# A two-layer AdaLN / Hyena / GQA / MoE kernel: queries and keys projected with features on partitions, and each head's operands fetched by way of HBM

## What is computed

```python
q = (hidden_states @ Wq).reshape(b, s, H, D).transpose(0, 2, 1, 3)
k = (hidden_states @ Wk).reshape(b, s, HKV, D).transpose(0, 2, 1, 3)
v = (hidden_states @ Wv).reshape(b, s, HKV, D).transpose(0, 2, 1, 3)
q = _apply_rope(q, cos, sin)          # re = xe*cos - xo*sin, ro = xe*sin + xo*cos
k = _apply_rope(k, cos, sin)
scores = jnp.einsum('bkgqd,bkpd->bkgqp', qg, k) * scale
scores = jnp.where(causal, scores, jnp.float32(-1e+30))
probs = jax.nn.softmax(scores, axis=-1)
out = jnp.einsum('bkgqp,bkpd->bkgqd', probs, v).reshape(b, H, s, D)
out = out.transpose(0, 2, 1, 3).reshape(b, s, H * D)
return out @ Wo
```

## Time and profile before

| | |
|---|---|
| median of 3 executions | 2249.2 us (2247.33 to 2249.74) |
| the profiled execution | 2249.1 us, its span 2247.3 us |
| mean granted TensorE clock | 0.931 |
| PE busy, weight loads busy | 1951.0 us (87%), 1739.9 us (77%) |
| DVE, ACT, POOL busy | 1338.3 (60%), 829.1 (37%), 508.1 us (23%) |
| moved by DMA | 70.77 MB |

### The profile page before, as it was taken

The page is one execution under the profiler, slowest core; times in us unless marked ns, Lnnn a source line. Parts: engine busy times, 40 slices in busy tenths (PEclk is TensorE's granted clock), DMA queues, the critical chain, the costliest instruction groups (busy, mean ns, idle before and its releaser), DMA issues.

```text
span 2247.3 us, 32490 instructions
## 1 busy us (share of the span) xinstructions
PE 1951.0 (87%) x11892; PEld 1739.9 (77%) x11892; DVE 1338.3 (60%) x3102; ACT 829.1 (37%) x1673; POOL 508.1 (23%) x991
## 2 busy tenths in 40 slices
PE   6868799999876789999976879999987688999997
PEld 4657699999755788999865769989976577999896
DVE  4598555553558755555358865555454985655535
ACT  1303444543321345445231334454422034444423
POOL 0051222121134221221016122212112421222101
PEclk8988899999988889999988889999998798999998
DMA  5400000000410000000050000000041000000005
GB/s 208 178 1 1 1 1 1 1 1 1 168 48 1 1 1 1 1 1 2 13 204 0 1 1 1 1 1 2 1 164 53 1 1 1 1 1 2 1 1 187
DMA packets 28522, 70.77 MB, mean 31 GB/s; under 512 B 4607, under 2 KB 19775, under 8 KB 24774
## 3 DMA queue, kind: packets, MB, share of 16 engines
q1 hardware_dynamic: 28358, 68.60, 8.3%
HBM read 58.35 MB, written 9.98 MB: 30 GB/s over the span
## 4 chain that ended last, share of the span: by engine, by line
PE 60%; DVE 20%; ACT 6%; issue 5%; DVEq 4%; DMA 2%; POOL 2%; POOLq 1%; SPq 1%; ACTq 0%
PE ps L454 20%; PE ps L300 8%; DVE ps L961 6%; PE ps L610 5%; PE ps L423 5%; PE ps L441 4%; PE ps L440 4%; PE ps L306 4%; PE ps L633 3%; PE ps L402 2%; ACT qhh L696 2%; DVE prod L1021 2%; DVE hrow L867 1%; DMA gate_scratch<-grow 1%; DVEq L1043 1%
## 5 line engine op out<-in xcount | busy, mean ns | idle before, releaser
L454 PEld LDWEIGHTS ps<-v,pT 128*128 128x128 f32 x4608 | 546.0, 192 | 12.6 <-ACT pT L713 1.9
L454 PE MATMUL ps<-v,pT 128*128 128x65 f32 x4608 | 538.4, 272 | 1.5 <-ACT pT L713 1.5
L713 ACT ACTIVATE pT<-ps 128x512 f32<-128x512 f32 (+3 forms) x768 | 332.7, 493 | 344.5 <-PE ps L441 332.7
L961 DVE CUSTOM_DVE_ANT_0 ps<-ps,mrow 128x128 f32<-128x128 f32 (+7 forms) x512 | 373.2, 784 | 39.5 <-PE ps L423 39.5
L1173 POOL TENSOR_SCALAR_AFFINE_SELECT pT<-pT 128x128 f32<-128x128 f32 x512 | 145.4, 292 | 928.7 <-ACT pT L713 922.9
L440 PE MATMUL ps<-qhh,khl 128*128 128x512 f32 (+3 forms) x768 | 275.8, 363 | 9.2 <-DMA q<-nmr 9.2
L441 PE MATMUL ps<-q,k 65*128 65x512 f32 (+3 forms) x768 | 261.9, 354 | 0.0
L423 PE MATMUL ps<-khl,qhh 128*128 128x512 f32 (+3 forms) x768 | 228.4, 379 | 36.9 <-DVE mx L961 14.8
L971 DVE RECIPROCAL den<-ps 128x4 f32<-128x4 f32 x128 | 23.4, 183 | 299.8 <-PE ps L454 299.8
L954 DVE TENSOR_TENSOR q<-ps,qhh 64x512 fp32r<-64x512 f32 x128 | 87.4, 683 | 186.6 <-ACT qhh L696 186.6
L672 ACT ACTIVATE hfull<-ps,modb 128x512 f32<-128x512 f32 x48 | 37.3, 776 | 434.4 <-PE ps L378 434.4
(11 more groups left out here) (162 smaller groups left out, 2854.4 us busy)
## 6 DMA issues: line engine op xcount, KB each, us to landing
sgn<-sgn_scratch SPq DMA_DIRECT2D x8, 1024.0 KB, 13.7
Kf<-kf_scratch SPq DMA_DIRECT2D x4, 2048.0 KB, 17.1
in_w<-in_w_scratch SPq DMA_DIRECT2D x4, 1536.0 KB, 10.7
x<-in_x SPq DMA_DIRECT2D x5, 1024.0 KB, 5.4
xn<-in_x SPq DMA_DIRECT2D x4, 1024.0 KB, 7.4
out<-x SPq DMA_DIRECT2D x4, 1024.0 KB, 5.0
wraw<-in_wmod SPq DMA_DIRECT2D x2, 1536.0 KB, 6.7
fwd<-in_fwd SPq DMA_DIRECT2D x5, 512.0 KB, 18.3
```

The source lines that it names most:

```text
L454: q = mm(ps[:, b, (i % 4) * (HD + 1):(i % 4 + 1) * (HD + 1)], pT[:, slot, i * P - lo:(i + 1) * P - lo], v1[:, g % 2, j, :], start=j == 0, ...
L713: A(pT[:, n % PRING, 0:(c + 1) * HALF - lo], ps[:, b, 0:(c + 1) * HALF - lo], ACT.Exp, scale=SCALE)\
L961: V.tensor_tensor_reduce(out=v, in0=v, in1=mrow[:, L - n:L], scale=1.0, scalar=-3e38, op0=ALU.add, op1=ALU.max, accum_out=mx[:, u % 2, i:i ...
```

## The change

1. The weights are laid out so that 128 output features are one half (even or odd rotary halves) of four heads: `project(k, col)` makes 128 features x 512 tokens, two such blocks (`e` = 0, 1) for a turn k, with 12 matmuls of 512 columns. Turns 0 and 2 are the keys of all four groups, turns 1 and 3 the queries of group 0, turns 4 to 9 those of groups 1 to 3; the latter are made during heads 1, 5 and 9. The values of all groups are projected in the prologue (`project_values`, 256 columns).
2. DVE multiplies a block by cosine and sine in one operation of 128x1024, POOL combines with two of 128x512, ACT (`high`) and DVE (`low`) split with one of 128x1024 each. All intermediate space is `oT`, `pT` and a tile `split`.
3. SP stores each turn (1 MB) into `q_scratch` or `k_scratch` in HBM and loads from there what a head needs: three DMAs of 256 KB for a query, 512 and 256 KB for a key. The loads for head u+1 wait until head u-1's exponentials are done, and stand ahead of head u's row of maxima on SP's queue. All transposes of queries and keys are gone, and so are ACT's and DVE's operations for single heads.
4. Storage: the rotary table grows from 256 KB to 1 MB, `zT`, `gabs` and `gsgn` move into other tiles, and two of the Hyena part's three product buffers become `hrow` and `vrow`; the second pooled product therefore waits for the last spectrum (`bk.wait(dve, ("vf", NB - 1))`).

```diff
+            def project(k, col):
+                for e in range(2):
+                    b = bk.take(pe, ("rope", k, e), until=(s["rope_a"], 2 * k + e + 1))
+                    h, c = k % 2 if k >= 4 else k // 2, col + e * P
+                    split_mm(ps[:, b, :], lambda a, q: wqkv[:, a, q, c:c + P],
+                             lambda a, q: hT[:, a, q, h * HALF:(h + 1) * HALF], ND).then_inc(ready[b], 1)
...
-                if i % 4 == 0:
-                    pe.wait_ge(s["q_done"], NHALF * u + i // 4 + 1)
-                    pe.wait_ge(s["k_lo_done"], NHALF * g + i // 4 + 1)
+                if u == 0 and i == 0:
+                    pe.wait_ge(s["first_loaded"], 16 * 5)
+                elif i == (0 if u else 4):
+                    pe.wait_ge(*q_loaded(u))
+                    if u % GQ == 0:
+                        pe.wait_ge(*k_loaded(g))
...
+            def high(k):
+                act.wait_ge(s["rope_done"], k + 1)
+                if k >= 3:
+                    act.wait_ge(*rope_stored({3: 0, 4: 2}.get(k, k - 1)))
+                A(split_of(k)[:, 0], turned(k)[:, 0:2, :], ACT.Copy).then_inc(s["rope_hi"], 1)
...
+            def low(k):
+                dve.wait_ge(s["rope_hi"], k + 1)
+                V.tensor_tensor(split_of(k)[:, 1], turned(k)[:, 0:2, :], split_of(k)[:, 0].bitcast(F32), ALU.subtract)\
+                    .then_inc(s["rope_lo"], 1)
...
+                def store(k):
+                    sp.wait_ge(s["rope_lo"], k + 1)
...
+                    dma(to.rearrange("x p n -> p x n"), split_of(k).rearrange("p a e n -> p (a e) n").bitcast(F32))\
+                        .then_inc(rope_stored(k)[0], 16)
+                def load_key(g, cols, done):
+                    one = k_scratch[:, g * 32:(g + 1) * 32, cols]
+                    dma(khl[:, g % 2, cols].bitcast(F32), one)\
+                        .then_inc(done, 16)
+                    dma(k2[0:HD, g % 2, cols].bitcast(F32), one[0:2]).then_inc(done, 16)
+                def load_query(u, cols, done):
+                    g, j, r = u // GQ, u % GQ, u % QRING
+                    one = q_scratch[g % 2, :, j * 32:(j + 1) * 32, cols]
+                    for half in (0, HD):
+                        dma(qhh[half:half + HD, r, cols].bitcast(F32), one[0:2]).then_inc(done, 16)
+                    dma(q2[0:HD, r, cols].bitcast(F32), one[2:4]).then_inc(done, 16)
+                for h in range(NHALF):
+                    cols = slice(h * HALF, (h + 1) * HALF)
+                    store(2 * h)
+                    store(2 * h + 1)
+                    sp.wait_ge(*rope_stored(2 * h))
+                    load_key(0, cols, s["k_loaded0"] if h else s["first_loaded"])
+                    sp.wait_ge(*rope_stored(2 * h + 1))
+                    load_query(0, cols, s["q_loaded0"] if h else s["first_loaded"])
+                every = slice(0, L)
+                load_query(1, every, s["q_loaded1"])
+                load_key(1, every, s["k_loaded1"])
                 for u in range(HEADS):
+                    w = u + 1
+                    if u:
+                        sp.wait_ge(s["exp_done"], 12 * u)
+                        if u % GQ == 0 and u // GQ + 1 < KV:
+                            load_key(u // GQ + 1, every, k_loaded(u // GQ + 1)[0])
+                        if w < HEADS:
+                            if w % GQ == 0:
+                                for k in range(2 * (w // GQ) + 2, 2 * (w // GQ) + 4):
+                                    sp.wait_ge(*rope_stored(k))
+                            load_query(w, every, q_loaded(w)[0])
                     sp.wait_ge(s["nmr_done"], u + 1)
-                    if u >= QRING:
-                        banks["batch"].wait(sp, ("pv", u - QRING, 1))
                     dma(q2[HD:HD + 1, u % QRING, :].bitcast(F32), nmr[:, u % 2, :].bitcast(F32))\
                         .then_inc(m_loaded(u)[0], 16)
+                    if u % GQ == 1 and u // GQ + 1 < KV:
+                        k = 2 * (u // GQ) + 4
+                        store(k)
+                    if u % GQ == 2 and u // GQ + 1 < KV:
+                        store(2 * (u // GQ) + 5)
```

More of the change, by code:

```diff
@@ L714, in exps, with value_rows @@
                     .then_inc(s["exp_done"], 1)
-            def value_rows(g, tiles=range(NT)):
-                for t in tiles:
-                    b = bk.wait(act, ("qkv", g, t))
-                    act.wait_ge(s["rot_a"], g * NT + t + 1)
-                    A(v1[:, g % 2, t, 0:HD], ps[:, b, QK:GW], ACT.Copy).then_inc(s["v_done"], 1)
+            def value_rows(h):
+                for t in range(4 * h, 4 * h + 4, 2):
+                    b = bk.wait(act, ("v", t))
+                    A(v1[:, :, t:t + 2, 0:HD].rearrange("p g t n -> p t g n"),
+                      ps[:, b, :].rearrange("p (t g n) -> p t g n", t=2, g=KV), ACT.Copy).then_inc(s["v_done"], 1)
             def turn_outputs(w):
+                act.wait_ge(s["rope_lo"], 4 if w < 4 else TURNS)
                 for h in range(NHALF):
@@ L896, in _ @@
             dve.wait_ge(s["loaded_raw"], 16 * 4)
-            split([wqkv[:, a, :, :, :].rearrange("p q g n -> p q (g n)") for a in range(2)], wraw[:, :, :])
+            split([wqkv[:, a, :, :] for a in range(2)], wraw[:, :, :])
             dve.drain()
@@ L1015, in _ @@
                     slot = 0 if pooled is None else 1 + pooled % 2
+                    if pooled == 1:
+                        bk.wait(dve, ("vf", NB - 1))
                     if pooled is not None and pooled >= 2:
@@ L1067, in _ @@
                     normed(LN_ATT, h, x)
-                rotate(0, range(2))
+                rotate(0)
                 h_low(LN_ATT, 1)
-                rotate(0, range(2, NT))
-                turn_head(0)
+                rotate(1)
+                low(0)
+                low(1)
+                rotate(2)
+                rotate(3)
+                low(2)
+                low(3)
                 for i in range(NT):
@@ L1083, in _ @@
                             row_maxima(w, i)
+                    if k:
+                        low(k)
                     normalise(u, 0)
@@ L1090, in _ @@
                         negate(w)
+                    if k:
+                        low(k + 1)
                     normalise(u, 1)
@@ L1225, in _ @@
                 pool.drain()
-                rotate(0)
+                for k in range(4):
+                    rotate(k)
                 for u in range(HEADS):
```

232 lines of the change are left out of this document (103 added, 129 removed).

## The result

The changed kernel takes 3369.6 us (median of 4 runs, 3363.3 to 3380.1) against 2249.5 for the kernel before on the same chip: ratio 1.498, 95% interval 1.494 to 1.503. The prediction was 3220, slower. Experiments 2, 3, 4, 6 and 7 were executed once each, the others 4 to 12 times.

What follows compares the result with a forecast made beforehand. The prediction took PE to bound the loop over heads. Two-engine loads would add 196 us in the heads and 47 in the prologue, 243 a batch, 971 for four on 2249.1, giving 3220 us, range 2780 to 3450.

Steps and rivals of the forecast that it cites:

- PE bounds the heads before, ACT's and DVE's savings count nothing: Loop over heads: PE busy 290.6 of 298.3 us in batch 1, so work taken off ACT and DVE gains nothing.
- The loads run on two engines: Query loads from HBM: two outer blocks put each on 2 of 16 engines, 15.4 us a query instead of 1.8.
- The row queues behind the query: SP's queue in the heads: the row of maxima lands only when the next head's query has, PE idle 11 us.
- E to S, 17.55 us: Between heads: from the last exponential, the query lands at 17.4 us and PE's first score product starts 0.15 later.
- S to E at the lower clock, 11.65 us: Within a head: first score product to last exponential, at the lower clock after PE's idle time, 11.65 us.
- rival 3: Two engines at the slower whole-span rate, 17.1 us a query: 3335 us; within the forecast's own range, no separate chance.
- Projections, three times 8 us: Heads that carry projections: three a batch at 8 us each, 24 us, partly at the lower clock.
- The prologue, 47 us: Ahead of head 0: stores and loads queue on the first engines, its start moves from 253.4 to 300.1, plus 47 us.
- S0 less the first projection: Sign in the prologue: first projection to head 0's first score product should take about 78 us, where it was 31.5.
- The sum: Whole kernel: 196 us in the heads and 47 in the prologue, 243 a batch, 971 for four, giving 3220.
- Rival 1: Heads: two engines but the row isn't held back, only the next head's score rows wait; 2830 us, chance 0.13.
- Rival 2: Loads use all 16 engines, so PE never waits for queries in the heads; 2205 us, chance 0.12.

Runs made afterwards that it cites:

- Experiments 2: Changed kernel with each head's row of maxima issued ahead of the next head's loads, still on two engines: 3203.2 us.
- experiment 3: Changed kernel with the row of maxima issued by ACT on a second queue, loads unchanged on SP's: 2892.4 us.
- experiment 4: Changed kernel with 40 filling products of 512 columns ahead of the wait for the row in heads 1 to 14: 3351.7 us.
- experiment 6: Changed kernel with 56 filling products of 512 columns ahead of the wait for the row in heads 1 to 14: 3206.2 us.
- 7: Changed kernel with the second of the three query loads left out from head 2 on: 3099.2 us.
- experiment 5: Changed kernel with loads spread (32 rows outermost) and the row of maxima issued ahead of the next head's loads: 2258.3 us, ratio 1.004 to the kernel before.
- the first experiment: Changed kernel with all query and key loads naming their 32 rows outermost instead of the blocks: 2278.6 us, ratio 1.013 to the kernel before.
- experiment 9: On experiment 5, DVE rotates turns 2 and 3 ahead of the low part of turn 1 in the prologue: 2266.3 us, ratio 1.008 to the kernel before.
- the repeat of 10: The same kernel as experiment 10, run again on one chip with the kernel before given a filled start: 2232.5 us, ratio 0.993 to the kernel before.
- experiment 10: On experiment 5, filling products in the four waits ahead of head 0's columns: 2232.4 us, ratio 0.991 to the kernel before.

## Why the prediction was right, point by point

- **PE bounds the heads before, ACT's and DVE's savings count nothing.** Held: in experiment 5, where no head waits for its row but head 0, the loop gains 14 us a batch of the 22 that PE's own savings were priced at, so none is left that ACT's or DVE's would have given. PE's first projection stands at 221.89 against 221.88, so storage and tables cost nothing up to there.
- **The loads run on two engines.** Held: 14 small packets and 2.06 engines busy at 25 GB/s (25.6 was taken), 56 and 3.7 us with the rows outermost. The reading of small packets as a count of engines, which was the whole of the evidence in the earlier trace rows, carried the forecast. The semaphore's count said nothing: a load on 2 engines raises it by 16 as well.
- **The row queues behind the query.** Held, and on the same engines: six of its eight pieces moved 2 us after its issue, the two others with the end of the loads. L452 has 60 waits and L436 none in the heads; a second queue takes 477 us off, one load fewer 4.8 a head.
- **E to S, 17.55 us.** Too short: 18.9 is the mean of 12 heads without a key (18.4 to 19.5), 29.6 and 28.9 at the keys where 27.8 was expected. Of the 1.4 us at a plain head 0.9 are the transfer: the loads' packets run from 321.44 to 337.74, 16.3 us for the 15.4 worked out. That is some 19 us a batch.
- **S to E at the lower clock, 11.65 us.** Mis-sized: 16.0 for head 0, and 11.9 to 16.1 in the eleven later heads without a projection, mean 13.7. The 11.65 was head 0 of the kernel before at clock 0.77, less its transposes. But the clock does not come back alike in every head. In all four batches the 28 heads that have output transposes between their columns took 11.9 to 13.4 us at a clock of 0.74 to 0.85, and the 20 that have neither these nor a projection (heads 0, 3, 7, 11 and 13) took 15.3 to 16.1 at 0.50 to 0.55, with PE busy nearly throughout. That is the case that rival 3 named, "a clock that stays low for the whole head". The length of the idle time ahead does not sort them: it is 12.4 us ahead of head 2 and 12.6 ahead of head 3. The head that the 11.65 came from had eight transposes between its columns, the ones that the change takes out, and the sum took off their time but kept the clock. That the transposes are what brings the clock back is my reading of this pattern; no run put them in or took them out alone. Net of the 10 us counted apart for the output transposes, and of 4 by which the three heads with a projection came out shorter than forecast, this is 13 a batch more.
- **Projections, three times 8 us.** Fair: the heads that carry one took 17.8 to 18.9 from S to E in batch 1, where 11.65 and 8 make 19.65.
- **The prologue, 47 us.** 50.7: the low parts of turns 0 to 3 ended at 235.9, 240.7, 247.8 and 251.3 (forecast 235.5, 239.2, 246.6, 249.2), head 0's second row group came at 277.5 (274.4), S0 at 304.1 (300.1). S0 less the first projection is 82.3, 78 was named.
- **The sum.** 33 us in the heads and 4 in the prologue are missing, 36.5 x 4 = 146, which is what lies between 3220 and the profiled 3368 to 2 us. The mechanism was right; the two terms that were too small are E to S, 19 us a batch, and S to E at the lower clock, 13.
- **Rival 1** is what experiment 3 shows, at 2892 where 2830 was worked out. **Rival 2** put 16 engines at 2205, and the first experiment shows 2279: its S0 came 17 us later, not 11 (the last low part ended at 253.4 where 249.2 was forecast, and SP spends 0.6 us on each issue), head 0 ran at the low clock, which it left out, and the row was still late in three heads, head 0 and the two behind a key. Its loop came near, 22 us a batch forecast: S0 to S15 takes 14 us less than before in experiment 5 and 16.5 less once the start is filled (means of four batches, 270.8 and 268.5 for 285.0).

## What to carry to other kernels

Look at the outermost dimension of both sides of a DMA: two blocks of a split tensor outermost, in place of their 32 rows, cost 1091 us here. The small packets of a transfer in the profile tell how many engines it used, before it hurts. A short transfer that gates an engine should not stand behind long ones in the same queue, and moving it ahead only helps if what it now delays is not in its own circle. And look for idle time ahead of dense PE work: the wait is paid once, the clock after it again.

## What the runs showed of the hardware that was not expected

- In experiment 4 the columns of head 1, after 9.34 us of dense products at the full clock and 3.28 us of idle time, ran at 1.2 GHz; without the idle time, in experiment 6, they ran at 2.4. It isn't a matter of length alone: in the same batch of experiment 4 head 6 kept a clock of 1.00 from S to E after 2.96 us of idle time (519.94 to 530.23), and head 5, after 2.80 us, did not (0.90). Filling 74% of a wait (9.34 of 12.6 us) gave 18 us of 3370, filling nearly all of it 163.
- PE can be busy for 16 us without getting its clock back: head 0 of the changed kernel was busy for 15.96 of 15.96 us at 0.52. The heads with output transposes, which have more to do, were the shorter ones (12.7 us for head 2, 15.7 for head 3). At the full clock, in experiment 6, it is the other way round: 10.2 and 9.5 us.
- A transfer of 4 KB issued on a second queue, while the first had three loads for the same two engines, landed in 5.07 us, more than the 1.9 of an idle queue and a third of 15.27.
- The spread versions scatter more from run to run (2245 to 2276 for experiment 5, 2227 to 2255 for the repeat of 10) than the kernel before on the same chips (2245 to 2255), and their time goes with the clock: the fastest execution of experiment 5 had a mean granted clock of 0.920, the slowest 0.907. The profiles show one way: a fall to 1.2 GHz without idle time ahead of it, as in experiment 9, some 8 us each. The profile of the repeat (2242.8 us) has one of them, that of experiment 10 (2267.3, 35 us above the median of its five) has four.
